# A vision tower in one kernel: one bf16 shift row per head, the range flag on VectorE, a rebuilt preparation, and embed and value projection in one piece each

## The chip, the core and the metric

The kernel runs on one core of one Trainium2 chip. The metric is the device time of one execution in microseconds, the median of several runs. One execution was recorded by the hardware profiler; what is said of durations comes from that record.

## What is computed

Sixteen images of 128 x 512 numbers are cut into 1024 patches of 64, embedded, passed through one attention layer with a bias per column, and through a mixture of eight experts of which each token takes two. Cut to what matters:

```python
h = patches(x) @ W.T + b + pos_embed              # 16 x 1024 x 64
y = layernorm(h)
q, k, v = y @ Wq + bq, y @ Wk + bk, y @ Wv + bv   # 8 heads of 8
col_bias = zeros(8, 1024).at[:, edge_index[1]].set((edge_attr @ We + be).T)   # the last edge of a node wins
attn = softmax(q @ k.T / sqrt(8) + col_bias[None, :, None, :])
h = h + (attn @ v) @ Wo + bo
t = layernorm(h)
p = softmax(t @ router_w.T); keep the two largest, divide by their sum
h = h + t + sum_e combine[:, e] * (gelu(t @ w1[e] + b1[e]) @ w2[e] + b2[e])
```

A softmax does not change when a number is subtracted from all scores of a row. The kernel makes use of that: it subtracts a bound (the shift) in place of the row's maximum, and has a slow path for an image whose bound is too large to be safe (its flag).

## The kernel before

The program has three stages: the **setup** (lines 720 to 1070), the **main loop** over 16 images, and the **expert stage** (64 units of work, four per image).

**Main loop.** An image is 32 quads. In quad q TensorE makes four score matmuls of 128 x 512 (`scores`, L1446: keys against queries, four heads, in two blocks of 1024 columns), ScalarE takes the exponential of both blocks (L1247), and TensorE multiplies the probabilities of quad q-2 by the values (`values`, L1462, four groups of 32 columns of the array side by side). The blocks go through three score buffers in PSUM, so a block's scores wait for the exponential of three blocks before. All other work of TensorE is put between the two, at most one piece in a quad: the table `AUX_SLOTS` names the quad, the step and its half. Pieces are the projection of queries and keys of the next image (`qk0`, `qk1`), the output projection, router and combine weights of the image before (`out_proj`, `post_t`, `router`, `combine_t`), the sums of squares of queries and keys (`sq`), the flag, the values of the next image (`v`), and embedding and transposition of the image after the next (`embed`, `norm_t`). All pieces write the same PSUM bank `aux`. So each step waits until VectorE has emptied the bank of the step before (`aux_drained`, in `aux_step`), and a waiting piece holds up the scores and values that stand behind it on TensorE.

VectorE runs its steps in the same order of quads (`body`, from L1355). Its own work sits at named quads: `evacuate` at quads 1, 9, 17 and 25 (it turns the summed values, L1315, and divides them, for the output projection), `centre_tokens` at 7, `scale_tokens` at 9, `rank_experts` at 20, `weigh_experts` at 22, `lead_centre` at 25, `normalise` at 27. `scale_tokens` waits for GpSimd, which takes the power -1/2 (L1187).

**The operands of the scores.** A score matmul has 54 rows: 48 hold the bf16 parts of queries and keys (three parts each, six products), three hold the column bias against ones, three hold the shift of the query (in three bf16 parts) against ones. Per image VectorE splits queries and keys into parts (L513 to L523), makes the shift of each query from its sum of squares and its head's bounds (`shift_of`, L536 to L553), SyncE stores parts and shift in DRAM and reads them back as rows (`store_parts`, `store_shift`, `load_rows`, `load_shift`). The flag of an image comes from a matmul over the heads (L697) and VectorE (L505); TensorE, ScalarE and VectorE read it when an image begins.

**Setup.** The winning edge of each node is found by matmuls of one-hot codes: VectorE makes `hot_b` and `hot_a` by 32 instructions each (L939, L942), TensorE sums them (L1047, 128 matmuls), VectorE finds the winners (L955 on), GpSimd gathers their attributes (L888). VectorE makes the bias, TensorE turns it (L1065), VectorE splits it into parts (L1023 on); ScalarE's queue stores the parts in DRAM and reads them as rows of `KA` (L845 to L851). GpSimd clears the values' tile `VA` (L877). The first image's embedding, projections and parts are made between these. At the end of the setup all engines meet.

```python
        dict(embed_0=7, embed_1=6, norm_t_0=2, qk0=3, qk1=4, v=7, sq=3, norm_t_1=2, flag=6)   # banks in the setup
```

Of the kernel before, what the change touches and what calls it, by code (L numbers as in the profile page):

```python
# [11 lines left out]
P = 128  # L12
# [40 lines left out]
HALVED = ["qk0", "qk1", "out_proj", "router", "v", "embed"]  # L53
LEAD = ["embed", "norm_t"]
PREP = ["qk0", "qk1", "v", "sq", "flag"]
POST = ["out_proj", "post_t", "router", "combine_t"]
FIRST_STEPS = ["embed_0", "embed_1", "norm_t_0", "qk0", "qk1", "v", "sq", "norm_t_1", "flag"]
FIRST_DRAINS = ["embed_0", "embed_1", "qk0", "qk1", "v", "sq", "norm_t_1", "flag"]
CENTRE_SLOT, SCALE_SLOT, LEAD_SLOT, NORM_SLOT = 7, 9, 25, 27
ROUTER_EXP_BLOCK = 38  # L60
# [61 lines left out]
def attention(nc, pool, io, psum, scratch, out):  # L122
    H_all, bmax, ident, ident_bf = (pool[k] for k in ("H_all", "bmax", "ident", "ident_bf"))
    q_parts_d, k_parts_d, shift_d, fb_d = (scratch[k] for k in ("q_parts", "k_parts", "shift", "fb"))
    x2_d, cT_d = scratch["x2"], scratch["cT"]
    ctx = ExitStack()
    with ctx:
# [58 lines left out]
        ones8 = sb("ones8", [H, 1], F32)  # L186
# [16 lines left out]
        sq = sb("sq", [P, BANK], F32)  # L203
# [5 lines left out]
        rq = sb("rq", [H, 1], F32)  # L209
        coef = sb("coef", [P, 4], F32)  # L210
        excess = sb("excess", [H, 1], F32)
        shift = sb("shift", [Q_ROWS, BANK], F32)
        shift_rest = sb("shift_rest", [Q_ROWS, BANK], F32)
        shift_parts = sb("shift_parts", [Q_ROWS, PARTS, BANK], BF16)
# [14 lines left out]
        def last_use(k):  # L229
# [6 lines left out]
                      dict(embed_0=7, embed_1=6, norm_t_0=2, qk0=3, qk1=4, v=7, sq=3, norm_t_1=2, flag=6).items()}  # L236
# [31 lines left out]
        excess_ready = sem("excess_ready")  # L268
# [3 lines left out]
        shift_stored = sem("shift_stored")  # L272
# [25 lines left out]
        EDGE_CHAIN = 25  # L298
        AUG_DMAS = 2 * 2 + 2
        PARTS_STORES = 16 * 12  # L300
        FB_SCORED, FB_MAXED, FB_MOVED, FB_CHAIN = FB_UNITS + 1, FB_UNITS + 1, 48, 4
        LEAD_CHAIN, PREP_CHAIN, POST_CHAIN, EVAC_CHAIN = 3, 13, 20, 5
# [20 lines left out]
        def sync_steps(sp):  # L323
# [1327 lines left out]
```

## Time and profile before

| | |
|---|---|
| median of 3 runs | 1176.12 us (1175.19 to 1176.16) |
| the profiled execution | 1175.44 us |
| its span, first to last instruction | 1173.6 us |
| TensorE matmul busy | 1105.3 us (94%) |
| ScalarE busy | 1030.7 us (88%) |
| VectorE busy | 671.2 us (57%) |
| GpSimd busy | 131.8 us (11%) |
| first scores of the main loop | at 55.5 us |
| last exponential of the main loop starts | at 1009.9 us |

The span is what the parts of the argument add up in; 1.84 us of the profiled execution lie around it. A busy TensorE here isn't TensorE at its limit, since it counts from the start of a matmul to its modelled end and the matmuls overlap. ScalarE's exponentials overlap as well. So the views in order of time say more than the shares.

### The profile page before, as it was taken

The page shows a single profiled execution, that of the slowest core. Times are in us where ns is not written, and L with a number is a line of the kernel's source. Part 1 is how long each engine was busy: PE and PEld are TensorE (multiplying, and loading weights), DVE is VectorE, ACT ScalarE, POOL GpSimd, SP SyncE. Part 2 cuts the span into 40 slices and gives each one's busy share as a digit, 9 for nine tenths or more (in the row PEclk, how much of TensorE's full clock was granted, in tenths as well). Part 3 has the DMA queues.
Part 4 walks back from the last instruction along what each step waited for, and adds up shares of the span by engine and source line. Part 5 has one row for each costly group of instructions (what it writes and reads, how often), then busy time and mean ns, then how long its engine had stood idle before and what let it go on. Part 6 is the DMA issues. An engine that isn't in the chain of part 4 may idle for free. (4 is left out here: it accounts for less than half of the span.)

```text
span 1173.6 us, 21907 instructions
## 1 busy us (share of the span) xinstructions
PE 1105.3 (94%) x7938; PEld 326.1 (28%) x7938; DVE 671.2 (57%) x1899; ACT 1030.7 (88%) x1127; POOL 131.8 (11%) x137
## 2 busy tenths in 40 slices
PE   3399999999999999999999999999999999899998
PEld 3122222222222222222222222222222222233332
DVE  9542756565656555565656565656565624367665
ACT  0199999999999999999999999999999999754553
POOL 4302201010101010101010101010101100000000
PEclk8589999999999999999999999999999999999999
DMA  2421323232323232323232323222222220022332
GB/s 52 111 74 39 85 53 82 53 83 53 83 53 84 53 83 53 83 49 87 49 88 49 86 50 73 63 68 67 62 67 55 72 61 10 16 63 66 84 75 50
DMA packets 63041, 75.93 MB, mean 65 GB/s; under 512 B 26338, under 2 KB 31458, under 8 KB 62906
## 3 DMA queue, kind: packets, MB, share of 16 engines
q1 hardware_dynamic: 60076, 73.01, 25.1%
q8 instruction: 80, 1.31, 0.5%
q10 hardware_dynamic: 2350, 1.10, 0.4%
q14 instruction: 55, 0.45, 0.1%
q0 software_dynamic: 480, 0.06, 0.1%
HBM read 37.54 MB, written 36.49 MB: 63 GB/s over the span
## 5 line engine op out<-in xcount | busy, mean ns | idle before, releaser
L1247 ACT ACTIVATE probs<-psum 128x1024 f32<-128x1024 f32 x1024 | 946.5, 1144 | 13.2 <-PE psum L1446 10.9
L1462 PE MATMUL psum<-probs,VA 128*32 128x512 f32 x4096 | 547.0, 606 | 5.3 <-DVE oT L1315 0.9
L1446 PE MATMUL psum<-QA,KA 54*128 54x512 bf16 x2048 | 331.7, 385 | 20.0 <-ACTq L1266 9.1
L1446 PEld LDWEIGHTS psum<-QA,KA 54*128 54x128 bf16 x2048 | 75.0, 93 | 491.5 <-ACT probs L1247 448.3
L1315 DVE STREAM_TRANSPOSE oT<-psum 128x512 f32<-128x512 f32 x64 | 45.9, 717 | 143.3 <-PE psum L1462 143.3
L1462 PEld LDWEIGHTS psum<-probs,VA 128*32 128x32 f32 x4096 | 82.1, 108 | 144.6 <-issue 86.1
L1282 ACT ACTIVATE probs<-psum,b 128x1024 f32<-128x1024 f32 x64 | 67.9, 1111 | 53.6 <-PE psum L1515 53.5
L1393 DVE TENSOR_TENSOR probs<-probs,psum 128x1024 f32<-128x1024 f32 x64 | 78.2, 1221 | 51.6 <-PE psum L1525 30.4
L484 DVE TENSOR_SCALAR qk<-psum,b_qk,scale_qk 128x512 f32<-128x512 f32 x32 | 25.8, 810 | 134.4 <-PE psum L673 134.4
L1515 PE MATMUL psum<-m_x,w 64*128 64x512 f32 x256 | 60.5, 591 | 1.5 <-ACT probs L1282 1.5
L1539 PE MATMUL psum<-probs,w 128*64 128x512 f32 x256 | 60.9, 598 | 0.0
L395 POOL COPY VA<-v_new 128x256 f32<-128x256 f32 x32 | 12.7, 397 | 426.1 <-DVE v_new L489 270.6
L1187 POOL TENSOR_TENSOR p_rstd<-p_ve,neg_half 128x8 f32<-128x8 f32 x16 | 32.3, 2020 | 230.5 <-DVE p_ve L430 230.5
L386 POOL TENSOR_TENSOR rstd<-ve,neg_half 128x8 f32<-128x8 f32 x16 | 31.6, 1974 | 123.4 <-DVE ve L430 123.4
L673 PE MATMUL psum<-xnT,w_qk 64*128 64x256 f32 x128 | 39.2, 407 | 0.8 <-ACT xnT L839 0.8
L1525 PE MATMUL psum<-m_cT,spread 64*128 64x512 bf16 x128 | 24.7, 382 | 6.4 <-DVE probs L1393 6.3
L661 PE MATMUL psum<-w_tok,xT 128*128 128x128 f32 x128 | 24.0, 317 | 6.7 <-DMA tok_b<-in_tok_b 6.7
L1515 PEld LDWEIGHTS psum<-m_x,w 64*128 64x128 f32 x256 | 24.3, 188 | 19.2 <-issue 15.2
L459 DVE TENSOR_TENSOR H_all<-psum,posb 128x512 f32<-128x512 f32 x16 | 11.1, 692 | 29.3 <-PE psum L661 29.2
L1289 ACT ACTIVATE yT<-psum 128x512 f32<-128x512 f32 x16 | 9.6, 597 | 20.2 <-PE psum L1539 20.2
L673 PEld LDWEIGHTS psum<-xnT,w_qk 64*128 64x128 f32 x128 | 24.7, 204 | 8.3 <-issue 1.9
L1320 DVE TENSOR_TENSOR oT_norm<-oT,o_inv 128x128 f32<-128x128 f32 x64 | 24.9, 389 | 2.3 <-DVE o_inv L1318 0.2
(175 smaller groups left out, 830.9 us busy)
## 6 DMA issues: line engine op xcount, KB each, us to landing
QA<-q_parts_d SPq DMA_DIRECT2D x64, 192.0 KB
KA<-k_parts_d SPq DMA_DIRECT2D x64, 192.0 KB
q_parts_d<-qk_parts SPq DMA_DIRECT2D x31, 192.0 KB, 2.5
k_parts_d<-qk_parts SPq DMA_DIRECT2D x31, 192.0 KB, 2.7
xT<-in_xT SPq DMA_DIRECT2D x16, 256.0 KB, 2.6
x_d<-x2T SPq DMA_DIRECT2D x16, 256.0 KB, 2.1
m_x<-x_d SPq DMA_DIRECT2D x16, 256.0 KB, 2.7
out_h<-result SPq DMA_DIRECT2D x16, 256.0 KB, 3.2
```

Source lines behind the costliest of these rows:

```text
L386: g.tensor_tensor(rstd[:, :], ve[:, :], neg_half[:, :], ALU.pow).then_inc(rstd_ready, 1)
L484: v.tensor_scalar(qk[:, n * BANK:(n + 1) * BANK], bank, b_qk[:, 0:1], scale_qk[:, 0:1], ALU.add, ALU.mult).then_inc(free, 1)
L673: last = pe.matmul(aux[:, cols], w_qk[rows, :, :].rearrange("k a e -> k (a e)"), xnT[rows, cols], start=True, stop=True)
L1187: g.tensor_tensor(p_rstd[:, :], p_ve[:, :], neg_half[:, :], ALU.pow).then_inc(p_rstd_ready, 1)
L1247: nc.scalar.activation(probs[:, k % PROB_BUFS, :], score_buf(buf_of(k)), ACT.Exp).then_inc(exped, 1)
L1282: nc.scalar.activation(act_h[:, u % H_BUFS, :], hid[u % 2], ACT.Gelu, bias=b1[:, u % PAIRS:u % PAIRS + 1]).then_inc(gelued, 1)
L1315: v.transpose(oT[:, :, :].rearrange("p j r -> p (j r)"), o_acc).then_inc(o_evacuated, 1)
L1393: v.tensor_tensor(gated[:, u % H_BUFS, :], act_h[:, u % H_BUFS, :], wgt, ALU.mult).then_inc(gated_ready, 1)
L1446: last = pe.matmul(score_buf(buf_of(k))[:, (g % 2) * BANK:(g % 2 + 1) * BANK], KA[rows_of(h, SCORE_ROWS), h // 2, jt * P:(jt + 1) * P], QA ...
L1462: last = pe.matmul(o_acc[32 * g:32 * g + 32, :], VA[:, jt, h, :], probs[:, k % PROB_BUFS, (g % 2) * BANK:(g % 2 + 1) * BANK], start=(jt == ...
L1515: last = pe.matmul(hid[u % 2][:, t * BANK:(t + 1) * BANK], w1[rows, m, :], m_x2[rows, b % 2, :], start=True, stop=True)
L1539: last = pe.matmul(ysum[D * t:D * (t + 1), :], w2[:, m, :], gated[:, u % H_BUFS, t * BANK:(t + 1) * BANK], start=False, stop=(m == PAIRS - 1))
```

## The change

- **Shift.** One bf16 number per head in place of three parts per query: minus the product of the largest norms of queries and keys of the head, not under -32. `shift_of` is one instruction on 8 x 1024, behind it `flag_of` makes the flag with a 32 x 32 transpose, a maximum and a comparison. Both stand at quad 14 on VectorE, behind quad 12's `sq`. The copy of the sums of squares, the shift's arithmetic and splitting, its round trip through DRAM and the flag's matmul are gone. `load_shift` copies the row from SBUF to SBUF, `load_zeros` writes zeros in the other two rows.
- **Quads.** The table of pieces and VectorE's own quads are changed; `embed` and `v` have one piece in place of two.
- **Setup.** The one-hot codes are made by three instructions over 4096 elements per partition. ScalarE clears `VA`. The bias's largest value is subtracted from the bias itself before it is split (`bias_tops`, `bmax`, `bias_low`), and its parts go from SBUF to the rows of `KA` directly, three DMAs on each of two queues (`place_bias`). The parts of heads 4 to 7 of the first image are stored in the main loop (`first_parts(sp, 1)`). Eight matmuls of 128 x 512 that nobody reads stand at the end of TensorE's setup, and TensorE waits for the bias's rows ahead of the loop.

```diff
-AUX_SLOTS = {0: ("qk0", 0), 1: ("qk0", 1), 2: ("qk1", 0), 4: ("qk1", 1), 6: ("out_proj", 0), 7: ("out_proj", 1),
-             10: ("sq", 0), 13: ("post_t", 0), 16: ("router", 0), 18: ("router", 1), 19: ("flag", 0), 20: ("v", 0),
-             21: ("v", 1), 23: ("embed", 0), 24: ("embed", 1), 26: ("combine_t", 0), 29: ("norm_t", 0)}
+AUX_SLOTS = {0: ("qk0", 0), 2: ("qk0", 1), 4: ("qk1", 0), 6: ("qk1", 1), 8: ("out_proj", 0), 10: ("out_proj", 1),
+             12: ("sq", 0), 14: ("post_t", 0), 16: ("router", 0), 18: ("router", 1), 21: ("embed", 0), 25: ("v", 0),
+             28: ("combine_t", 0), 30: ("norm_t", 0)}
-CENTRE_SLOT, SCALE_SLOT, LEAD_SLOT, NORM_SLOT = 7, 9, 25, 27
-ROUTER_EXP_BLOCK = 38
+CENTRE_SLOT, SCALE_SLOT, SHIFT_SLOT, LEAD_SLOT, NORM_SLOT = 10, 12, 14, 23, 26
+ROUTER_EXP_BLOCK = 40
-COMBINE_SLOT, WEIGH_SLOT = 20, 22
+COMBINE_SLOT, WEIGH_SLOT = 20, 25
...
+            def load_shift(bp, hg):
+                sp.wait_ge(shift_ready, bp + 1)
+                for par in range(2):
+                    r = HALF_ROWS * par + SHIFT_ROW
+                    heads = slice(4 * hg + par, 4 * hg + 4, 2)
+                    sp.dma_start(QA[r:r + 1, 2 * hg:2 * hg + 2, :].rearrange("o h i -> o (h i)"),
+                                 shift_row[heads, :]).then_inc(aug_loaded[hg], 16)
...
+            def shift_of(bp, st):
+                v.wait_ge(rq_ready, bp + 1)
...
+                v.tensor_scalar(shift_row[:, :], minus_ones[:, :], rq[0:H, 0:1], -RQ_CLIP, ALU.mult,
+                                ALU.max).then_inc(shift_ready, 1)
...
-                    for n in range(32):
-                        v.tensor_scalar(hot_b[:, n, :], node_bf[:, :], float(n), exp_bits[:, 0:1].bitcast(F32),
-                                        ALU.is_equal, ALU.mult)
-                    for n in range(32):
-                        last = v.tensor_scalar(hot_a[:, n, :], node_af[:, :], float(n), None, ALU.is_equal)
-                    last.then_inc(hot_ready, 1)
+                    each = digits[:, :, :].unsqueeze(1).broadcast_to([P, EC // 2, 32, 2])
+                    in_pairs = "p (m t) -> p m t"
+                    nodes_b = node_bf[:, :].rearrange(in_pairs, t=2).unsqueeze(2).broadcast_to([P, EC // 2, 32, 2])
+                    nodes_a = node_af[:, :].rearrange(in_pairs, t=2).unsqueeze(2).broadcast_to([P, EC // 2, 32, 2])
+                    link(v.tensor_tensor(hot_b[:, :, :, :], nodes_b, each, ALU.is_equal))
+                    v.tensor_scalar(hot_b[:, :, :, :], hot_b[:, :, :, :], exp_bits[:, 0:1].bitcast(F32), None, ALU.mult)
+                    v.tensor_tensor(hot_a[:, :, :, :], nodes_a, each, ALU.is_equal).then_inc(hot_ready, 1)
+                    v.memset(ones3[:, :], 1.0).then_inc(ones_ready, 1)
+                    v.memset(zeros[:, :], 0.0).then_inc(ones_ready, 1)
...
-                    g.wait_ge(hot_ready, 1)
-                    g.memset(VA[:, :, :, :], 0.0).then_inc(room_set, 1)
...
+                    for n in range(WARM_MATMULS):
+                        pe.matmul(first_bank["qk1"], ident_bf[:, :],
+                                  hot_b[:, 0:8, :, :].rearrange("p m b t -> p (m b t)"), start=True, stop=True)
...
+                pe.wait_ge(bparts_moved, 96)
                 all_batches(pe, body)
```

What moved, at the three places of which the prediction speaks. First, **VectorE around quads 9 to 13** of an image (`oT`, `o_inv` and `oT_norm` are the evacuation, `h` the output projection, `x` and `H_all` `scale_tokens`, `sq_max` the emptying of the bank after `sq`). Before:

```order
L430 TENSOR_SCALAR p_ve<-p_mv 128x8
L433 TENSOR_TENSOR p_centred<-h,p_mv 128x512
L1315 STREAM_TRANSPOSE oT<-psum 128x512
L1318 RECIPROCAL o_inv<-oT 128x16
L1320 TENSOR_TENSOR oT_norm<-oT,o_inv 128x16x8
L574 TENSOR_TENSOR x<-p_centred,p_rstd 128x2x4x64
L576 TENSOR_TENSOR H_all<-h,x 128x512
L498 COPY sq<-psum 128x512
L499 TENSOR_REDUCE sq_max<-psum 128x1
```

Now:

```order
L1314 STREAM_TRANSPOSE oT<-psum 128x512
L1317 RECIPROCAL o_inv<-oT 128x16
L1319 TENSOR_TENSOR oT_norm<-oT,o_inv 128x16x8
L575 TENSOR_TENSOR h<-psum,H_all 128x512
L419 BN_STATS p_stats<-h 128x6 x8
L425 BN_AGGR p_mv<-p_stats 128x2 x8
L427 TENSOR_SCALAR p_ve<-p_mv 128x8
L430 TENSOR_TENSOR p_centred<-h,p_mv 128x512
L563 TENSOR_TENSOR x<-p_centred,p_rstd 128x2x4x64
L565 TENSOR_TENSOR H_all<-h,x 128x512
L495 TENSOR_REDUCE sq_max<-psum 128x1
```

The output projection stands behind the evacuation of quad 9 now, and `scale_tokens` straight in front of `sq`'s maximum; the copy of `sq` is gone. Before, the maximum stood there too, but the output projection was three quads earlier.

Second, **TensorE at quads 20 to 24** before (each quad is four scores, a piece or none, and values; `w_v` marks `v`, `w_tok` marks `embed`):

```order
L1446 MATMUL psum<-QA,KA 128x512 x4
L677 MATMUL psum<-w_v,xnT 128x128 x2
L1462 MATMUL psum<-probs,VA 32x512 x4
L1446 MATMUL psum<-QA,KA 128x512 x4
L677 MATMUL psum<-w_v,xnT 128x128 x2
L1462 MATMUL psum<-probs,VA 32x512 x4
L1446 MATMUL psum<-QA,KA 128x512 x4
L1462 MATMUL psum<-probs,VA 32x512 x4
L1446 MATMUL psum<-QA,KA 128x512 x4
L661 MATMUL psum<-w_tok,xT 128x128 x2
L1462 MATMUL psum<-probs,VA 32x512 x4
L1446 MATMUL psum<-QA,KA 128x512 x4
```

and at quads 25 to 28 now:

```order
L1448 MATMUL psum<-QA,KA 128x512 x4
L666 MATMUL psum<-w_v,xnT 128x128 x4
L1464 MATMUL psum<-probs,VA 32x512 x4
L1448 MATMUL psum<-QA,KA 128x512 x4
L1464 MATMUL psum<-probs,VA 32x512 x4
L1448 MATMUL psum<-QA,KA 128x512 x4
L1464 MATMUL psum<-probs,VA 32x512 x4
L1448 MATMUL psum<-QA,KA 128x512 x4
L696 MATMUL psum<-ident_bf,comb_parts 128x128 x4
L1464 MATMUL psum<-probs,VA 32x512 x4
```

`v` is one piece of four matmuls with two quads without a piece behind it, and `combine_t` follows in the third.

Third, **VectorE behind the router**, where the experts' weights are made (`rank` is the last of the ranking, the weights begin with `chosen` and end, ten instructions later, in `comb_parts`). Before, at quads 21 and 22:

```order
L626 TENSOR_REDUCE rank<-above 128x64
L489 TENSOR_TENSOR v_new<-psum,b_v 128x512
L632 SCALAR_TENSOR_TENSOR chosen<-rank,rprob 128x64
L634 TENSOR_REDUCE c_sum<-chosen 128x8
L635 TENSOR_SCALAR c_inv<-c_sum 128x8
L636 RECIPROCAL c_sum<-c_inv 128x8
```

Now, at quad 25:

```order
L1314 STREAM_TRANSPOSE oT<-psum 128x512
L1317 RECIPROCAL o_inv<-oT 128x16
L1319 TENSOR_TENSOR oT_norm<-oT,o_inv 128x16x8
L486 TENSOR_TENSOR v_new<-psum,b_v 128x512
L621 SCALAR_TENSOR_TENSOR chosen<-rank,rprob 128x64
L623 TENSOR_REDUCE c_sum<-chosen 128x8
L624 TENSOR_SCALAR c_inv<-c_sum 128x8
```

The weights (`chosen` and the ten instructions behind it) stood behind the `v` of quad 21, ahead of the evacuation of quad 25; they stand behind that evacuation now.

## Rows read from the trace of the kernel before

**Rows 1.** The page, clock of TensorE in 40 slices, tenths of full speed

```profile
PEclk8589999999999999999999999999999999999999
```

**Rows 2.** Timeline of ScalarE, image 5: start, us, engine, line, what, count [idle before]

```profile
404.02 17.52 ACT L1247 ACTIVATE probs<-psum 128x1024 f32<-128x1024 f32 x19 [0.24 <-PE psum L1446]
```

**Rows 3.** The exponentials' own view: duration ns shortest/median/longest, first and last start

```profile
L1247 ACT ACTIVATE probs<-psum x1024: 1017/1136/1581, 56.2 to 1009.9; 128x1024 f32<-128x1024 f32 x171
```

**Rows 4.** Timeline of GpSimd, the same step in two images after each other

```profile
373.70 2.02 POOL L1187 TENSOR_TENSOR p_rstd<-p_ve,neg_half 128x8 f32<-128x8 f32 x1 [11.54 <-DVE p_ve L430]
...
433.25 2.02 POOL L1187 TENSOR_TENSOR p_rstd<-p_ve,neg_half 128x8 f32<-128x8 f32 x1 [11.54 <-DVE p_ve L430]
```

**Rows 5.** Timeline of TensorE, image 5, quads 21 to 25

```profile
395.53 0.60 PE L1446 MATMUL psum<-QA,KA 54*128 54x512 bf16 x4
396.07 0.71 PE L677 MATMUL psum<-w_v,xnT 128*128 128x128 f32 x4
...
397.71 0.61 PE L1446 MATMUL psum<-QA,KA 54*128 54x512 bf16 x4
398.24 1.06 PE L1462 MATMUL psum<-probs,VA 128*32 128x512 f32 x8
399.24 0.60 PE L1446 MATMUL psum<-QA,KA 54*128 54x512 bf16 x4
...
403.59 0.39 PE L1446 MATMUL psum<-QA,KA 54*128 54x512 bf16 x2
```

**Rows 6.** Timeline of TensorE, image 5, a transposing piece

```profile
410.92 0.66 PE L667 MATMUL psum<-ident,xn 128*128 128x128 f32 x4
```

**Rows 7.** Timeline of VectorE, image 5, from the output projection to the combine parts

```profile
370.79 0.69 DVE L586 TENSOR_TENSOR h<-psum,H_all 128x512 f32<-128x512 f32 x1 [0.51 <-PE psum L701]
...
374.98 0.72 DVE L1315 STREAM_TRANSPOSE oT<-psum 128x512 f32<-128x512 f32 x1 [0.77 <-PE psum L1462]
...
376.34 0.68 DVE L574 TENSOR_TENSOR x<-p_centred,p_rstd 128x512 f32<-128x512 f32 x1
...
377.67 0.69 DVE L498 COPY sq<-psum 128x512 f32<-128x512 f32 x1
378.27 0.68 DVE L499 TENSOR_REDUCE sq_max<-psum 128x1 f32<-128x512 f32 x1
...
397.72 0.69 DVE L489 TENSOR_TENSOR v_new<-psum,b_v 128x512 f32<-128x512 f32 x1
398.33 0.22 DVE L632 SCALAR_TENSOR_TENSOR chosen<-rank,rprob 128x64 f32<-128x64 f32 x1
...
400.64 0.21 DVE L646 COPY comb_parts<-comb_parts 128x192 bf16<-128x192 bf16 x1
```

**Rows 8.** Timeline of all engines, the one-hot codes and what follows on them

```profile
3.65 5.30 DVE L939 TENSOR_SCALAR hot_b<-node_bf,exp_bits 128x128 bf16<-128x128 bf16 x32
...
8.86 3.35 DVE L942 TENSOR_SCALAR hot_a<-node_af 128x128 bf16<-128x128 bf16 x32
12.11 4.64 DVE L947 TENSOR_TENSOR posb<-posb,tok_b 128x512 f32<-128x512 f32 x1
...
12.27 4.61 PE L1047 MATMUL psum<-hot_b,hot_a 128*32 128x32 bf16 x128 [3.47 <-DVE hot_a L942]
...
19.63 1.22 DVE L955 SCALAR_TENSOR_TENSOR key<-psum,base 128x1024 int32<-128x1024 int32 x1
...
33.67 0.69 DVE L516 TENSOR_TENSOR squares<-qk_parts 128x1024 bf16<-128x1024 bf16 x1
```

**Rows 9.** Timeline of all engines, from the bias parts to the first scores

```profile
44.59 0.28 DVE L1023 CAST bparts<-psum 64x128 bf16<-64x128 f32 x1
...
49.48 0.62 SPq L360 DMA_DIRECT2D shift_d<-shift_parts  x2
...
55.53 1.04 PE L1446 MATMUL psum<-QA,KA 54*128 54x512 bf16 x4 [9.12 <-ACTq L1266]
```

**Rows 10.** Waits of ScalarE from 58 to 70 us: us in total, times, longest

```profile
ACT probs L1247 <- PE psum L1446: 2.8, 2, 1.9
```

More of the change, by code:

```diff
@@ L208, in attention @@
         rq2 = sb("rq2", [H, 1], F32)
[L209 to L214, printed above, removed]
+        rq = sb("rq", [32, 32], F32)
+        rq_turned = sb("rq_turned", [32, 32], F32)
+        rq_top = sb("rq_top", [1, 1], F32)
+        shift_row = sb("shift_row", [H, T], BF16)
         flags = sb("flags", [1, NB], I32)
@@ L502, in prep_step, with flag_of @@
                     square_bounds(link)
-                    shift_of(bp, link, close)
-                elif step == "flag":
-                    v.tensor_scalar(flags[0:1, ds(bp, 1)], bank[0:1, 0:1], 1.0, None,
-                                    ALU.min).then_inc(free, 1)
-                    v.wait_ge(free, freed)
-                    v.sem_inc(flag_ready, 1)
+            def shift_of(bp, st):
+                v.wait_ge(rq_ready, bp + 1)
+                if later(bp):
+                    for hg in range(2):
+                        v.wait_ge(aug_loaded[hg], 16 * AUG_DMAS * bp)
+                    alone(v)
+                v.tensor_scalar(shift_row[:, :], minus_ones[:, :], rq[0:H, 0:1], -RQ_CLIP, ALU.mult,
+                                ALU.max).then_inc(shift_ready, 1)
+            def flag_of(bp, st):
+                link, close = st["link"], st["close"]
+                link(v.transpose(rq_turned[:, :], rq[:, :]))
+                link(v.reduce_max(rq_top[:, :], rq_turned[0:1, 0:H], AX.X))
+                close()
+                v.tensor_scalar(flags[0:1, ds(bp, 1)], rq_top[:, :], RQ_LIMIT, None,
+                                ALU.is_gt).then_inc(flag_ready, 1)
             def split_high(bp, link):
+                if bp == 1:
+                    v.wait_ge(first_stored[1], PARTS_STORES // 2)
                 if bp > 1:
@@ L693, in aux_step @@
                                              squares[:, i * BANK:(i + 1) * BANK], start=True, stop=True)
-                elif step == "flag":
-                    pe.wait_ge(excess_ready, n + 1)
-                    alone(pe)
-                    last = pe.matmul(aux[0:1, 0:1], excess[:, :], ones8[:, :], start=True, stop=True)
                 elif step == "out_proj":
@@ L808, in _ @@
                     load_rows(0)
[L809 to L810 removed]
+                    place_bias(sp, 0)
                     sp.wait_ge(ones_placed, 64)
@@ L1047, in _ @@
                         last = pe.matmul(sums[tile:tile + 32, 32 * (m // 4):32 * (m // 4) + 32],
-                                         hot_a[:, :, m], hot_b[:, :, m], start=True, stop=True)
+                                         hot_a[:, m // 2, :, m % 2], hot_b[:, m // 2, :, m % 2], start=True, stop=True)
                         if m % 32 == 31:
@@ L1364, in body @@
                             scale_tokens(b - 1, st)
+                        if slot == SHIFT_SLOT and b + 1 < NB:
+                            shift_of(b + 1, st)
+                            flag_of(b + 1, st)
                         if slot == LEAD_SLOT and b + 2 < NB:
```

217 lines of the change are left out of this document (99 added, 118 removed).

## The prediction

> **What bounds the kernel now.** I read the page first, then ScalarE in order of time, then TensorE and VectorE quad by quad, then the setup. In the main loop ScalarE is the bound. It ends an exponential every 0.916 us: 19 of them span 17.52 us, less the 1.02 that one takes alone, over 18 [rows 2, 3]. 64 of them are 58.62 us, and the image takes 59.55, the distance of one and the same GpSimd step in two images [rows 4]. So 0.93 us an image are lost; about 0.14 of that is the router's exponential, which stays, and the rest is ScalarE waiting for scores, as the 0.24 at quad 25 shows [rows 2].
>
> TensorE is close behind. A quad without a piece takes it 1.53 us (397.71 to 399.24), against 1.83 for ScalarE's two exponentials; with half a `v` it takes 2.18 (395.53 to 397.71), so half a piece costs 0.65 and an empty quad gives back 0.30 [rows 5]. How late may TensorE be? The two blocks' scores start 0.22 apart (four take 0.61, two 0.39), and an exponential starts 0.43 behind its scores (403.59 to 404.02) [rows 2, 5]. The second block's scores start when an old exponential ends; the next quad's first exponential has to end four steps, 3.66 us, later, so its scores must start 3.66 - 1.02 - 0.43 = 2.21 after that moment. TensorE would be there after 1.53 - 0.22 = 1.31. The **lead is thus 0.9, less about 0.05 for the signal: 0.85 us** (an estimate). What a piece or a wait takes beyond it, less 0.30 per empty quad, is lost to ScalarE for good. The same rule over all quads of the kernel before gives 0.84 an image where 0.93 are measured, so I add 0.09 to what it says below.
>
> Ahead of the loop stand 55.5 us of setup, a chain of steps. And TensorE runs at half its clock, 1.2 GHz, around the start of the loop (the 5 in the second slice) [rows 1], which leaves ScalarE waiting for 2.8 us in image 0 [rows 10].
>
> **Setup: one-hot codes.** Sixty-four instructions took 5.30 + 3.35 us [rows 8]. Now three go over 4096 elements each. A two-source bf16 instruction of 1024 elements takes 0.69 [rows 8]; with some 0.15 of start, 4096 take 2.3 us. For the product with one source, each of the 32 `hot_a` instructions took 0.105 for 128 elements, mostly start, so I take 1.2 and 2.3 as its other end. Sum 2.3 + 1.2 + 2.3 = 5.8, a gain of 2.9. The nearest row is of plain rows of memory, though, and these instructions read each pair of nodes 32 times over; were they to take one element per cycle, twice 2.1 us would come back (a rival below).
>
> The Trainium skill ("Vector Engine (DVE) Microarchitecture Reference", 5.1 Performance modes) has two-source instructions make two results a cycle if all types are 16-bit and the innermost dimension is dense with more than one element. A pair is such a dimension, so by the page the 2.3 stands; it also reports one element read again and again at one result a cycle, which is the rival's case.
>
> **Setup: the bank and the port.** `posb` took 4.64 us, beside GpSimd's clearing of `VA`; the same shape takes 0.69 elsewhere (`h`) [rows 7, 8]. ScalarE clears `VA` now, in time where it only waits. So the additions, the first embedding and its statistics fit beside TensorE's 4.61 us of sums: codes ready at 9.3, sums at 14.0, VectorE there at about 14.2 (some 1.5 for two memsets of 1536 elements in all, at the 512 in 0.69 of `h`; 0.7 for `posb`; 2.8 for the rest, as from its end at 16.75 to 19.63). `key`, at 19.63, starts **5.4 us earlier** [rows 8]. What follows on it, winners, gather, bias, is a chain without change up to one more copy (0.25) and then a maximum and a subtraction (0.65).
>
> **Setup: its end.** The parts began at 44.59 [rows 9]; now 44.59 - 5.4 + 0.25 + 0.65 = 40.1, done at 41.3. Before, shift arithmetic up to 49.48 and two hops through DRAM followed, 6.05 us to the first scores at 55.53 [rows 9]. Now one hop remains: three small DMAs per queue and a landing, some 3.3 us, 44.6; TensorE then reads the flag and branches, 1.1 us. First scores at 45.7, **a gain of 9.8**. The bounds are 7 (a hop of 4, codes late by 2) and 11.5. What SyncE's queue sheds from the setup, the parts of heads 4 to 7, is needed at quad 16, 29 us later: no cost. The eight spare matmuls take 3.4 at half clock and end by 44, behind the bias: no cost.
>
> **The clock at the start.** They may make the clock rise earlier. Bounds 0 and the 2.8 of [rows 10]; since TensorE idles for a microsecond or two behind them, and quads 0 and 1 hold no values, I take **1.0**.
>
> **Main loop: whole pieces.** Four matmuls in place of two add 0.44 to the 0.65 (four passes in the 0.71 of [rows 5], less 0.27 of the last): 1.09; the other bound is 2 x 0.65 = 1.30. Over the lead of 0.85 this loses 0.24 in quad 25. In quad 21 the router's exponential, just ahead on ScalarE, gives most of it back: 0.10. The losses of before (out_proj in adjacent quads, `v` in 20 and 21, `embed` in 23 and 24) go. Were this all, an image would gain some 0.4 us. The flag's matmul and the shift's arithmetic on VectorE were hidden: nothing.
>
> **Main loop: the wait in quad 14.** The bank must be emptied of `sq` before `post_t`, and on VectorE that maximum stands behind `scale_tokens`, which waits for GpSimd. Counted from quad 10's scores: evacuation of quad 9 begins at 0.2 (its values end about then: 1.06 from their start [rows 5]); +1.36 to `h`; +4.93 to the end of GpSimd's power (370.79 to 375.72); `x` at once and +1.33 to the next bank read; +0.68 and a signal: 8.55 [rows 4, 7]. Transposing and values add 0.6 and 1.0 [rows 5, 6]: quad 15's scores start 10.15 after quad 10's. Allowed are five quads, 9.16, plus the lead left, 0.85 - 0.65 + 0.30 = 0.50. **Lost 0.5.** Before, the bank was free three quads earlier. Queued behind the waiting piece are two quads' values and scores, hence ScalarE.
>
> **Main loop: quads 26 to 28.** From quad 26's scores, which have no lead after `v`: the evacuation begins at 0.2; its transpose (0.72) frees the sums at 1.0, so quad 27's scores come at 2.0, not 1.83: 0.18 lost. Then 1.36 for the evacuation, 0.61 `v_new`, 2.52 for the weights [rows 7]: `comb_parts` at 4.7. The piece (0.4) and values (1.0) bring quad 29's scores to 6.1; allowed are 2.0 + 3.66. **Lost 0.45.**
>
> Together 0.10 + 0.24 + 0.5 + 0.18 + 0.45 + 0.14 + 0.09 = 1.70, against 0.93: **+0.8 us an image**. Thirteen images have all of it, 10.4; image 14 (no embedding) about 0.9, image 0 (nothing of an image before) -0.2: **+11.1**. The expert stage is untouched.
>
> **Sum.** 1173.6 - 9.8 - 1.0 + 11.1 = 1173.9 of span, with the 1.84 around it 1175.7, against 1175.44 of the profiled execution and 1176.12 as median: no change. About 0.2% (2.35 us) is what a measurement of this kernel can tell from none.
>
> **Rivals.**
> - *The two waits don't bite.* If VectorE came 0.8 us sooner at both places, only the whole pieces would count: 1175.4 - 10.8 - 14 x 0.4 = 1159. For it: nothing idle is on those chains but GpSimd's 2.02. Against: each term is a row. Chance 0.07; half of it (1168) 0.13.
> - *The waits run longer.* TensorE's whole pieces at 1.30 add 0.2 twice an image, or signals on the chains 0.2 more each: +5.6, 1181.3. It decides as soon as an image takes over 60.5 us. Chance 0.17.
> - *One-hot codes at one element per cycle*: +4.2, 1179.9, if both comparisons take over 4 us each. Chance 0.08.
> - *The clock rises with the spare matmuls and stays*: -1.8 and a faster end of setup, 1173. Chance 0.12.
>
> My own case has 0.43. Its bounds and the rivals give 1168 to 1182; I hold the low end at 1170, leaving out the first rival. Faster 0.34 (the first and fourth rival and some of my case), same 0.38, slower 0.28.
>
> **What would show it.** First scores near 45.7; the three code instructions 2.3, 1.2, 2.3; `posb` 0.7; the same GpSimd step 60.3 apart in two images; `post_t` on TensorE waiting some 0.9 for VectorE's `sq_max`, and `combine_t` some 0.8 for `comb_parts`. An image of 59.2 would refute the waits; first scores after 48 would refute the setup.

## The result, and the profile after

| | before | after |
|---|---|---|
| median | 1176.12 us (1174.67 to 1176.65, 11 runs) | 1178.47 us (1178.12 to 1179.55, 11 runs) |
| ratio to before | | 1.0025, 95% interval 1.0017 to 1.0032 |
| the profiled execution, its span | 1175.44, 1173.6 us | 1178.41, 1176.3 us |
| first scores, first exponential | 55.53, 56.18 | 47.16, 47.59 |
| image 0, from its first exponential's end to the next image's | 62.54 | 60.75 |
| an image of the main loop | 59.55 | 60.51 |

The change is slower by 0.25%, a little more than the 0.2% within which I had called it no change (1175.7). The time is inside the range.

**Setup.** The timeline of the changed kernel, all engines (start us, us, engine, line, what); it answers to [rows 8]:

```profile
3.79 2.29 DVE L930 TENSOR_TENSOR hot_b<-node_bf,digits 128x4096 bf16<-128x4096 bf16 x1
...
6.11 1.29 DVE L931 TENSOR_SCALAR hot_b<-hot_b,exp_bits 128x4096 bf16<-128x4096 bf16 x1
...
7.32 2.28 DVE L932 TENSOR_TENSOR hot_a<-node_af,digits 128x4096 bf16<-128x4096 bf16 x1
...
9.65 1.29 PE L1042 MATMUL psum<-hot_b,hot_a 128*32 128x32 bf16 x128 [0.83 <-DVE hot_a L932]
...
11.13 0.62 DVE L938 TENSOR_TENSOR posb<-posb,tok_b 128x512 f32<-128x512 f32 x1
...
14.63 1.22 DVE L946 SCALAR_TENSOR_TENSOR key<-psum,base 128x1024 int32<-128x1024 int32 x1
```

The codes take 5.86 us in place of 8.65, `posb` 0.62 in place of 4.64, and `key` starts at 14.63, 5.0 us earlier (14.2 was predicted). TensorE's 128 matmuls on the codes take 1.29 us, where they took 4.61 before [rows 8]. How `posb` lay among its neighbours before (the same view of the kernel before) matters for the account below:

```profile
12.27 4.49 PEld L1047 LDWEIGHTS psum<-hot_b,hot_a 128*32 128x32 bf16 x128 [3.77 <-DVE hot_a L942]
...
12.34 5.81 POOL L877 MEMSET VA<- 128x2048 f32 x1 [9.43 <-DVE hot_a L942]
...
16.79 0.69 DVE L459 TENSOR_TENSOR H_all<-psum,posb 128x512 f32<-128x512 f32 x1
```

Then the end of the setup, which answers to [rows 9]:

```profile
41.09 0.28 DVE L1024 TENSOR_TENSOR bparts<-b_rest,bparts 64x128 bf16<-64x128 f32 x1
...
41.41 2.10 ACTq L778 DMA_DIRECT2D KA<-bparts  x3
...
47.16 0.61 PE L1448 MATMUL psum<-QA,KA 54*128 54x512 bf16 x4 [3.08 <-issue]
...
47.59 5.61 ACT L1246 ACTIVATE probs<-psum 128x1024 f32<-128x1024 f32 x6 [23.76 <-PE psum L1448]
```

and the view of the tile `bparts` (duration ns shortest/median/longest, first and last start; then the time from issue to landing):

```profile
L778 ACTq DMA_DIRECT2D KA<-bparts x3: 602/613/822, 41.4 to 42.9; - x3
...
DMA to landing us min/median/max: 2.5/2.8/3.2
```

The parts are ready at 41.4 as predicted. The last of the six small DMAs is issued at 42.9 and lands 2.6 later, at 45.5, and the first scores come 1.6 behind that: 5.8 us from the parts to the scores, where I had 4.4.

**The clock.** The page's row, against [rows 1]:

```profile
PEclk9699999999999999999999999999999999999999
```

The 6 is the slice from 29.4 to 58.8 us. In it the granted clock is at half from 30.6 to 44.2 and again from 47.7 to 54.5 us: TensorE starts the loop at full clock, falls back within a microsecond, and is back for good at 54.5.

**Main loop.** GpSimd's step in two images, which answers to [rows 4], is 60.51 apart:

```profile
372.39 2.02 POOL L1185 TENSOR_TENSOR p_rstd<-p_ve,neg_half 128x8 f32<-128x8 f32 x1 [17.23 <-DVE p_ve L427]
...
432.90 2.02 POOL L1185 TENSOR_TENSOR p_rstd<-p_ve,neg_half 128x8 f32<-128x8 f32 x1 [17.23 <-DVE p_ve L427]
```

The timeline of ScalarE over image 5 shows where it loses time. Behind each bracket ScalarE waited for scores; a run of x11 exponentials takes 10.19, which is 0.916 for each but the last:

```profile
378.67 10.19 ACT L1246 ACTIVATE probs<-psum 128x1024 f32<-128x1024 f32 x11 [0.56 <-PE psum L1448]
388.63 0.36 ACT L1251 ACTIVATE router_e<-logits 128x64 f32<-128x64 f32 x1
388.78 12.50 ACT L1246 ACTIVATE probs<-psum 128x1024 f32<-128x1024 f32 x13
401.44 3.77 ACT L1246 ACTIVATE probs<-psum 128x1024 f32<-128x1024 f32 x4 [0.17 <-PE psum L1448]
405.52 10.19 ACT L1246 ACTIVATE probs<-psum 128x1024 f32<-128x1024 f32 x11 [0.31 <-PE psum L1448]
```

The distances of the ends of the exponentials, quad by quad, less 2 x 0.916, as a mean of images 1 to 13:

```
quad      7    14   19/20  21   23   24   25   26   28   sum
before  0.15    -   0.14  0.23 0.05 0.34   -    -    -   0.91
after     -   0.67  0.14  0.12   -    -  0.25 0.27 0.42  1.87
```

The waits of the changed kernel (us in total, times, longest), the two of the prediction among them:

```profile
PE psum L672 <- DVE sq_max L495: 12.4, 14, 1.0
...
PE psum L696 <- DVE comb_parts L635: 8.8, 14, 0.6
...
PE psum L1464 <- DVE oT L1314: 7.7, 16, 0.5
```

`post_t` (L672) waits 0.87 an image for `sq_max`, and `combine_t` (L696) 0.63 for `comb_parts`: both new waits are there. The chain to quad 14 in image 5, TensorE and then VectorE:

```profile
367.92 0.61 PE L1448 MATMUL psum<-QA,KA 54*128 54x512 bf16 x4
...
376.69 0.63 PE L672 MATMUL psum<-ident,x 128*128 128x128 f32 x4 [0.87 <-DVE sq_max L495]
377.24 1.07 PE L1464 MATMUL psum<-probs,VA 128*32 128x512 f32 x8
378.24 0.60 PE L1448 MATMUL psum<-QA,KA 54*128 54x512 bf16 x4
```

```profile
368.13 0.72 DVE L1314 STREAM_TRANSPOSE oT<-psum 128x512 f32<-128x512 f32 x1 [1.12 <-PE psum L1464]
...
369.49 0.68 DVE L575 TENSOR_TENSOR h<-psum,H_all 128x512 f32<-128x512 f32 x1
...
374.52 0.69 DVE L563 TENSOR_TENSOR x<-p_centred,p_rstd 128x512 f32<-128x512 f32 x1 [1.61 <-POOL p_rstd L1185]
...
375.85 0.68 DVE L495 TENSOR_REDUCE sq_max<-psum 128x1 f32<-128x512 f32 x1
```

From quad 10's scores (367.92) to quad 15's (378.24) it is 10.32; I had 10.15. And quads 25 to 29, TensorE and then VectorE:

```profile
396.82 1.16 PE L666 MATMUL psum<-w_v,xnT 128*128 128x128 f32 x8
...
398.91 0.61 PE L1448 MATMUL psum<-QA,KA 54*128 54x512 bf16 x4
400.01 1.06 PE L1464 MATMUL psum<-probs,VA 128*32 128x512 f32 x8 [0.50 <-DVE oT L1314]
401.01 0.60 PE L1448 MATMUL psum<-QA,KA 54*128 54x512 bf16 x4
...
403.78 0.38 PE L696 MATMUL psum<-ident_bf,comb_parts 128*128 128x128 bf16 x4 [0.63 <-DVE comb_parts L635]
...
405.09 0.60 PE L1448 MATMUL psum<-QA,KA 54*128 54x512 bf16 x4
```

```profile
399.15 0.72 DVE L1314 STREAM_TRANSPOSE oT<-psum 128x512 f32<-128x512 f32 x1 [2.33 <-PE psum L1464]
...
403.42 0.21 DVE L635 COPY comb_parts<-comb_parts 128x192 bf16<-128x192 bf16 x1
```

### The profile page after: what moved, and what is told of

It is laid out like the page before. It is cut to its first block and busy times, and to the rows that moved or that the text cites. A ratio compares the mean times of both kernels' runs of the same rounds, so it can differ in the third digit from the quotient of the medians.

```text
span 1176.3 us, 21673 instructions
## 1 busy us (share of the span) xinstructions
PE 1093.9 (93%) x7913; PEld 319.5 (27%) x7914; DVE 611.9 (52%) x1700; ACT 1033.8 (88%) x1127; POOL 126.8 (11%) x137
## 3 DMA queue, kind: packets, MB, share of 16 engines
q8 instruction: 79, 1.29, 0.5%
## 5 line engine op out<-in xcount | busy, mean ns | idle before, releaser
L1517 PE MATMUL psum<-m_x,w 64*128 64x512 f32 x256 | 60.5, 591 | 1.5 <-ACT probs L1281 1.5
L462 DVE COPY xnT<-psum 128x512 f32<-128x512 f32 x15 | 10.4, 690 | 47.4 <-PE psum L656 47.4
L597 DVE TENSOR_REDUCE r_sum<-router_e 128x8 f32<-128x64 f32 x16 | 3.5, 220 | 54.0 <-ACT router_e L1251 54.0
L650 PE MATMUL psum<-w_tok,xT 128*128 128x128 f32 x128 | 20.4, 307 | 7.5 <-DMA tok_b<-in_tok_b 6.7
```

Source lines behind the costliest of these rows:

```text
L1517: last = pe.matmul(hid[u % 2][:, t * BANK:(t + 1) * BANK], w1[rows, m, :], m_x2[rows, b % 2, :], start=True, stop=True)
```

## The experiments

Each is the changed kernel with the edit named; the ratio is to the kernel before, run beside it on the same chip. In the first four only quads are changed. The kernel before took 1176.64 us beside e1 to e4, 1176.13 beside e5 to e8 and 1176.00 beside e9 to e11, so a difference of medians across these groups, or to the changed kernel's 1178.47, holds to about half a microsecond.

| | edit | median us | ratio, 95% interval | an image |
|---|---|---|---|---|
| e1 | `scale_tokens` a quad later | 1169.56 | 0.9940, 0.9924 to 0.9957 | 59.84 |
| e2 | `weigh_experts` a quad earlier | 1174.93 | 0.9985, 0.9976 to 0.9995 | 60.20 |
| e3 | quads of before | 1166.34 | 0.9908, 0.9892 to 0.9925 | 59.55 |
| e4 | `embed`, `v` in halves again | 1178.72 | 1.0022, 1.0013 to 1.0032 | 60.50 |
| e5 | no spare matmuls | 1179.12 | 1.0024, 1.0015 to 1.0034 | 60.49 |
| e6 | wait for the bias behind the flag | 1177.72 | 1.0014, 1.0004 to 1.0023 | 60.49 |
| e7 | a piece in every second quad | 1154.72 | 0.9816, 0.9800 to 0.9832 | 58.81 |
| e8 | e7 and e6 | 1153.53 | 0.9808, 0.9791 to 0.9824 | 58.81 |
| e9 | e8, bias parts leave one by one | 1153.79 | 0.9809, 0.9793 to 0.9825 | 58.81 |
| e10 | e9, 16 spare matmuls | 1154.71 | 0.9818, 0.9802 to 0.9835 | 58.81 |
| e11 | e8 again, beside e9 and e10 | 1152.99 | 0.9805, 0.9789 to 0.9821 | 58.81 |

My theory was that the new quads cost about 0.8 us an image through two waits and the whole pieces, and that the setup gives 9 to 10 back. The rivals were that the whole pieces alone cost it, and that the loss has to do with the new shift on VectorE.

**e1, the wait in quad 14.**

```diff
-CENTRE_SLOT, SCALE_SLOT, SHIFT_SLOT, LEAD_SLOT, NORM_SLOT = 10, 12, 14, 23, 26
+CENTRE_SLOT, SCALE_SLOT, SHIFT_SLOT, LEAD_SLOT, NORM_SLOT = 10, 13, 14, 23, 26
```

> The changed kernel with scale_tokens at quad 13 in place of 12, so that on VectorE the bank of sq is emptied ahead of it. In the changed kernel's profile an image takes 60.5 us and quad 14 loses 0.67 of that. Theory (TensorE's post_t waits for VectorE's sq maximum, which waits behind scale_tokens for GpSimd): the wait of post_t on sq_max goes, an image takes 59.8, the kernel about 9 us less (1169.5), and quads 25 to 28 keep their loss. Rival A (the transposing piece itself is what loses, whatever it waits for): an image stays at 60.5, 1178.5. Rival B (post_t then waits as long for x2, which GpSimd delays): a wait of some 0.8 for x2, 60.4.

`sq_max` stands ahead of `scale_tokens` on VectorE now, so the bank is empty before GpSimd's power is. TensorE's `post_t` has no idle time before it any more:

```profile
373.89 0.66 PE L672 MATMUL psum<-ident,x 128*128 128x128 f32 x4
```

The loss at quad 14 is 0, all others are as they were, and the time is 8.9 us shorter. The two profiles' spans differ by 8.7: images 1 to 14 are 9.65 shorter together, and in this profile the setup ended 0.8 later and image 0 took 0.15 more. So this wait alone costs about 9 us.

**e2, the wait in quad 28.**

```diff
-COMBINE_SLOT, WEIGH_SLOT = 20, 25
+COMBINE_SLOT, WEIGH_SLOT = 20, 24
```

> The changed kernel with weigh_experts at quad 24 in place of 25, ahead of the evacuation. Theory (combine_t in quad 28 waits for comb_parts, which stand behind evacuation and v): the wait on comb_parts goes, but v's bank and the evacuation may come later by what the weights take, so an image gains 0.2 to 0.4 us (60.1 to 60.3), the kernel 3 to 6 us (1172.5 to 1175.5). Rival (quads 25 to 28 lose because v is in one piece): an image gains nothing, 1178.5.

The 0.42 of quad 28 is gone and the time is 3.5 us shorter. Of the 0.42, 0.12 comes back at quad 26, since the weights stand ahead of the evacuation now and values wait longer for the transpose of the sums (`oT`, 7.7 before):

```profile
PE psum L1464 <- DVE oT L1314: 9.2, 16, 0.7
```

**e3, the quads of before** (table and VectorE's quads as before the change, the new shift at quad 11, the new setup kept).

```diff
+AUX_SLOTS = {0: ("qk0", 0), 1: ("qk0", 1), 2: ("qk1", 0), 4: ("qk1", 1), 6: ("out_proj", 0), 7: ("out_proj", 1),
+             10: ("sq", 0), 13: ("post_t", 0), 16: ("router", 0), 18: ("router", 1), 20: ("v", 0), 21: ("v", 1),
+             23: ("embed", 0), 24: ("embed", 1), 26: ("combine_t", 0), 29: ("norm_t", 0)}
+CENTRE_SLOT, SCALE_SLOT, SHIFT_SLOT, LEAD_SLOT, NORM_SLOT = 7, 9, 11, 25, 27
...
```

> The changed kernel (its setup, shift row and flag) with the quads of the kernel before, VectorE's own included, the shift at quad 11, v and embed in two pieces. Theory (the quads alone cost the main loop about 0.95 us an image; shift and setup only gain): an image back at 59.5, the kernel 1164 to 1167, which is 9 to 12 us under the kernel before. Rival (the shift row's DMAs, or the flag on VectorE, cost time in the main loop): an image stays above 60, 1174 or more.

Setup, shift and flag together are worth about 10 us: 10.3 against the kernel before beside it (1176.64 less 1166.34), 9.8 against its first median (1176.12). The image is 59.55 to the hundredth, with the losses of before in their old quads. So the shift and the missing flag matmul cost and bring nothing in the loop, and the new quads cost the other 12.1 (1178.47 less 1166.34), net of what they bring in image 0.

**e4, two pieces in place of one** (`embed` at 20 and 21, `v` at 24 and 25).

```diff
-             12: ("sq", 0), 14: ("post_t", 0), 16: ("router", 0), 18: ("router", 1), 21: ("embed", 0), 25: ("v", 0),
+             12: ("sq", 0), 14: ("post_t", 0), 16: ("router", 0), 18: ("router", 1), 20: ("embed", 0), 21: ("embed", 1),
+             24: ("v", 0), 25: ("v", 1),
-HALVED = ["qk0", "qk1", "out_proj", "router"]
+HALVED = ["qk0", "qk1", "out_proj", "router", "v", "embed"]
```

> The changed kernel with embed in quads 20 and 21 and v in quads 24 and 25, two pieces each, which end in the same quads as the whole pieces, so VectorE's order is the same. Theory (a whole piece costs 1.09 against 1.30 for two halves, but in one quad; both lose about as much over a lead of 0.85): an image within 0.2 of 60.5, the kernel 1176 to 1181. Rival (putting them in one piece is what costs): an image 0.5 or more shorter, 1171 or less.

Quad 21 loses 0.23 in place of 0.12 and quad 25 0.15 in place of 0.25: the sum is the same. One piece or two in adjacent quads makes no difference, which rules out the first rival. Whether it is their neighbourhood that counts, this run can't say; e7 takes them apart.

**e5, without the spare matmuls** (`WARM_MATMULS` 8 to 0).

> The changed kernel without the eight spare matmuls. Theory (they raise TensorE's clock for the loop's first microseconds, where the changed kernel lost 1.3 us in image 0 against 3.1 before): the granted clock is 1.2 GHz from the first scores on, image 0 takes 61.5 to 62.5 in place of 60.75, and since the engines meet perhaps 0.3 us sooner, the kernel is 0.5 to 1.5 us longer (1179.0 to 1180.0). Rival (qk0's second half moved out of quad 1 is what image 0 gained): image 0 stays at 60.8, the kernel at 1178.5 or under.

Image 0 takes 61.20, not 61.5 or more. The total is in the expected range but can't be told from the changed kernel's (ratios 1.0024 and 1.0025). Image 0 loses 0.46 more than in the changed kernel's profile, at quads 3 and 4. That isn't shown to be the spare matmuls' doing: in e2, which has all eight and the same first quads, image 0 takes 61.20 too and loses the same 0.46 there. In this trace the granted clock reads 1.00 throughout, though the matmuls tell otherwise; its first record of the clock is at 56.3 us, and the view shows what lies ahead of it as full:

```profile
52.59 1.94 PE L1464 MATMUL psum<-probs,VA 128*32 128x512 f32 x8
54.46 1.04 PE L1448 MATMUL psum<-QA,KA 54*128 54x512 bf16 x4
55.42 1.48 PE L1464 MATMUL psum<-probs,VA 128*32 128x512 f32 x8
56.84 0.60 PE L1448 MATMUL psum<-QA,KA 54*128 54x512 bf16 x4
```

Eight matmuls of values took 1.94 where they take 1.06 later, and four scores 1.04 where they take 0.60 two quads on: half clock, up to about 56.3. In the changed kernel the scores at 47.16 were at full pace, 0.21 apart, the granted clock was at half from 47.7 to 54.5, and then full. In the runs with the new first quads, what goes with the loss at quads 3 and 4 is how late the clock comes back behind the first values: 2.0 to 2.9 us in the changed kernel, e4, e6, e8 and e11, which lose 0.05 or nothing there, 3.1 and 3.4 in e1 and e7 (0.15 and 0.29), and 3.7 in e2 and e5 (0.46). All of these but e5 have the eight spare matmuls.

**e6, the wait for the bias behind the read of the flag.**

```diff
                     flag = pe.value_load(flags[0:1, ds(b, 1)], min_val=0, max_val=1)
+                    if b == 0:
+                        pe.wait_ge(bparts_moved, 96)
...
-                pe.wait_ge(bparts_moved, 96)
                 all_batches(pe, body)
```

> The changed kernel with TensorE's wait for the bias's rows moved behind its load of image 0's flag. In the changed kernel the last rows land at 45.5, and TensorE loads the flag and branches for 1.6 us behind that, first scores at 47.2. Theory (that order is most of the 1.4 us by which the end of the setup was sized too small): first scores near 46.0, the kernel 1.0 to 1.4 us less (1177.2). Rival (TensorE would wait as long for other loads or ScalarE): first scores at 47.2 again, 1178.5.

The first scores start at 46.36, 0.54 behind the last landing in place of 1.64. So 1.1 us of the start was TensorE's wait for the flag and its reading of it, which could as well run ahead of the wait for the bias; the branch on the flag still stands behind both, in the 0.54. By the medians 0.75 us of it arrived. In the profiles the first scores are 0.8 earlier, since the landing itself was at 45.82, 0.3 later than in the changed kernel's. The ratios' intervals overlap (1.0004 to 1.0023, and 1.0017 to 1.0032), so the clearer measure is e8 against e7 on one chip, 1.2.

**e7, a piece in every second quad**, and e8, the same with the late wait.

```diff
+             12: ("sq", 0), 14: ("post_t", 0), 16: ("router", 0), 18: ("router", 1), 20: ("v", 0), 22: ("v", 1),
+             24: ("embed", 0), 26: ("embed", 1), 28: ("combine_t", 0), 30: ("norm_t", 0)}
+HALVED = ["qk0", "qk1", "out_proj", "router", "v", "embed"]
+CENTRE_SLOT, SCALE_SLOT, SHIFT_SLOT, LEAD_SLOT, NORM_SLOT = 10, 13, 14, 27, 29
+COMBINE_SLOT, WEIGH_SLOT = 20, 23
```

> The changed kernel with a piece in every second quad: v in two pieces at quads 20 and 22, embed at 24 and 26, scale_tokens at 13, weigh_experts at 23, lead_centre at 27, normalise at 29. Theory (a half piece of 0.65 is inside the lead of 0.85 and the next quad gives back 0.30, and both of VectorE's late steps are gone): only the router's exponential is left, an image takes 58.8 to 59.0, the kernel 1153 to 1157. Rival (a loss that I do not know of comes in its place, a piece waiting for the bank of the piece two quads before): 59.4 or more, 1163 or more.

> The spaced quads together with the late wait. Theory: the two gains add, since one is in the setup and one in the loop: 1.0 to 1.4 us under the spaced kernel, 1152 to 1156. Rival (the two overlap, as image 0 waits for the slow clock anyway): as the spaced kernel.

By the rule of the prediction half a piece costs 0.65, within the lead of 0.85, and the empty quad behind it gives 0.30 back, so no quad should lose anything. ScalarE in image 5 of e7, start, us, count:

```profile
349.12 32.37 ACT L1246 ACTIVATE probs<-psum 128x1024 f32<-128x1024 f32 x35
381.07 0.55 ACT L1251 ACTIVATE router_e<-logits 128x64 f32<-128x64 f32 x1
381.22 31.59 ACT L1246 ACTIVATE probs<-psum 128x1024 f32<-128x1024 f32 x34
```

No idle time is left; only the router's exponential takes its 0.14. An image is 58.81, and the time is 21 us under the kernel before and 24 under the changed one; with the late wait another 1.2. The rule of the lead forecast this run (58.8 to 59.0 an image, 1153 to 1157 us), which is its strongest support. The run moves pieces and VectorE's steps at once, so it doesn't say what each move is worth.

**e9, the bias parts leave one by one** (to e8).

```diff
-                eng.wait_ge(bparts_ready, 1)
                 for a in range(PARTS):
+                    eng.wait_ge(bparts_ready, a + 1)
...
                     link(v.tensor_copy(bparts[:, 0, :], bias_low[:, :]))
+                    v.sem_inc(bparts_ready, 1)
...
                     link(v.tensor_copy(bparts[:, 1, :], b_rest[:, :]))
+                    v.sem_inc(bparts_ready, 1)
```

> The version with a piece in every second quad and the late wait, and each of the three bf16 parts of the bias leaves for KA as soon as VectorE has made it, in place of all three behind the last. In the changed kernel the parts are ready at 40.5, 41.1 and 41.4, the six DMAs are issued from 41.4 to 43.5, and the last lands at 45.5. Theory (the last hop is bound by issue of three DMAs in a row on each queue, 0.6 each, and then one landing of 2.6): issues from 40.6 on, the last by 42.7, lands at 44.7, first scores at 45.2, against 46.1: faster by 0.6 to 1.0, median 1152.5 to 1153.0. Rival (the landing is bound by something else, by the parts of the first image that are loaded at the same time): the last landing stays at 45.4 or later and the time within 0.3 of 1153.5.

The rival holds. The same view as above:

```profile
L778 ACTq DMA_DIRECT2D KA<-bparts x3: 602/638/770, 40.6 to 42.1; - x3
...
DMA to landing us min/median/max: 3.7/4.0/4.4
```

The DMAs are issued 0.8 us earlier and take 1.2 longer to land: the last lands at 45.87. The third part itself was ready 0.2 later than in the other runs, at 41.6, with two more signals ahead of it. The share of the DMA engines from 39 to 47 us, in slices of 0.2 us, in the changed kernel and in e9:

```profile
DMA  3885979999997999999865422110001989989989
```

```profile
DMA  3788959999999999999999982000001989989999
```

From about 40 the engines are full, to 43.0 us in the changed kernel and to 43.8 in e9, with the rows of `QA` and `KA` of the first image, four loads that SyncE issued from 37.6 to 40.2. The bias's own packets run from 42.6 to 44.35 in the changed kernel and from 42.95 to 44.0 in e9: so the 0.8 us of earlier issue is spent in waiting for the engines, as the rival has it. That the rows are the cause is read from this view, since the loads weren't taken away. But it isn't the whole hop. The engines are idle from 44.4 (44.0 in e9) to 45.0, and the last landing comes 1.2 us (changed kernel) and 1.85 us (e9) behind the bias's last packet. What that last stretch waits for no run shows.

**e10, 16 spare matmuls** (to e9).

> As the run with the early parts, and 16 spare matmuls in place of 8. With 8 the records show them 0.43 apart at half clock and 0.21 at full clock from 42.1 to 44.1 on, and the scores at half clock again from 47.5. Theory (the clock falls because TensorE does nothing between the spare matmuls and the first scores): 8 more take 1.7 to 3.4, so they end between 43.9 and 47.3; if they end at about 45, the four scores of quad 0 and on stay 0.21 apart, image 0 loses nothing at quad 2 (1.32 before), and the time is 0.8 to 1.3 shorter, 1151.3 to 1152.0. Rival (the clock falls again whatever is ahead of it, since the first two quads hold few matmuls): quad 2 loses over 1, and the spare matmuls delay the first scores by 0 to 2: 1152.5 to 1154.5.

The rival holds here too. TensorE in e10:

```profile
40.89 3.95 PE L1067 MATMUL psum<-hot_b,ident_bf 128*128 128x512 bf16 x15 [0.22 <-issue]
46.79 0.61 PE L1450 MATMUL psum<-QA,KA 54*128 54x512 bf16 x4 [1.94 <-ACTq L1267]
...
51.52 1.93 PE L1466 MATMUL psum<-probs,VA 128*32 128x512 f32 x8
```

The spare matmuls end at 44.8 and the first scores are at full pace, as in e9 (46.48). The granted clock falls again at 48.1 in e9 and at 48.8 in e10, ahead of the first values, and quad 2 loses 1.3 in both. The first scores are 0.3 later, and image 0 takes 60.79 against 60.60. Against e11 (image 0 60.12) both are slower by 0.8 to 1.7, so more of them is no gain. The difference of the three in image 0 is at quads 3 and 4 (0.48 in e9, 0.67 in e10, 0 in e11), and the clock comes back 3.8, 4.1 and 2.3 us behind the first values.

## Why the prediction was right or wrong

Term by term, in the span: what was predicted, and what the two profiles show.

| | predicted | measured |
|---|---|---|
| setup to the first exponential | -9.8 | -8.6 |
| image 0 | -1.2 | -1.8 |
| images 1 to 13 | +10.4 | +12.2 |
| image 14 | +0.9 | +1.35 |
| the rest | 0 | -0.5 |
| sum | +0.3 | +2.65 |

**Right: the mechanisms of the loop.** In the setup the durations up to the bias parts came about as worked out: codes 2.29, 1.29 and 2.28 against 2.3, 1.2 and 2.3, `posb` 0.62 against 0.7, parts done at 41.4 against 41.3. The codes read each pair 32 times over and were no slower for it: 4096 elements in 2.29 us is the pace of the 1024 in 0.69 [rows 8], and twice that of 512 f32 elements in 0.69 [rows 7]. By the Trainium skill's rule ("Vector Engine (DVE) Microarchitecture Reference", 5.1 Performance modes) such 16-bit operands make two results a cycle, and the trace agrees.

One term of the setup came right by luck, another for a reason that isn't shown. The 1.5 for the two memsets isn't what its row gives (1536 elements at 512 in 0.69 are 2.1); they took 0.91 and 0.48. And `posb` is short now, but that GpSimd's clearing had stretched it isn't shown. Before, it ended at 16.75, with TensorE's weight loads of the sums (12.27 + 4.49 = 16.76), while the clearing ran on to 18.15, and beside that clearing `H_all`, one of whose operands is in PSUM, took its usual 0.69. The change takes both neighbours away: ScalarE clears `VA`, and the new layout of the codes, in which the 32 numbers that a matmul reads from each partition lie 4 bytes apart in place of 256, went with sums of 1.29 us in place of 4.61, a term that the prediction had kept. No run separates the two. Nor did the shorter sums matter, since VectorE reaches `key` only at 14.63.

In the loop the six places of the losses are those named, the rule of the lead gives their sizes, and e1, e2 and e3 take away one after the other what it says. The rival of waits that don't bite is refuted by the 0.87 and 0.63 of idle time.

**Wrong: sizes, by three steps.** First, "one hop remains: three small DMAs per queue and a landing, some 3.3 us, 44.6; TensorE then reads the flag and branches, 1.1 us". The hop measured 4.1 and the start 1.64. Neither the 3.3 nor the 1.1 had a row behind it. I had taken the landing for the DMAs' own; e9 shows that the bias's packets wait for DMA engines that are full with the first image's rows, though the last 1.2 us to the landing stay open. That is 1.4 of the 9.8, of which a first exponential 0.43 behind its scores, in place of 0.65, gives 0.2 back.

Second, "lost 0.5" in quad 14, where it was 0.67. The chain was summed with `x` "at once" behind GpSimd's power and 0.05 for the signal to TensorE. The rows show 0.11 (372.39 + 2.02 to 374.52) and 0.16 (375.85 + 0.68 to 376.69), 0.22 more; the piece and the values then took 0.05 less than I had. Likewise at quad 26, where the evacuation begins 0.24 behind the scores in place of 0.2, and TensorE starts at 400.01, 0.14 behind the transpose's end at 399.87, in place of 0.08: 0.27 and not 0.18. Together that is 0.26 an image, less the 0.09 that I had added for what the rule didn't explain, which wasn't needed: with image 14, in which the same waits stand, 2.2 us. It is the second rival's mechanism ("signals on the chains 0.2 more each"), at 0.26 an image in place of its 0.4, about two thirds of its price of 5.6; only net of the 0.09 is it 2.2. That rival was to decide from 60.5 us an image, and the image is 60.51.

Third, the "1.0" for the clock. Image 0 gained 1.8, but most of it not by the clock: with the quads of before it takes 62.70 (e3), spare matmuls and all, and without the matmuls but with the new quads 61.20 (e5). At half clock scores and values alone take TensorE longer than ScalarE's 1.83 (from 52.59 to 55.42 in e5), a piece adds to it, and the new table spreads the first four pieces over quads 0 to 6. That is 1.3 to 1.5, and I had nothing for it: the 0.2 was for the pieces of later quads, which lose 0.80 in image 0 against 0.78 before. The other 0.3 to 0.5 goes with the clock's earlier return. That the spare matmuls bring it isn't shown, since e2 has them and takes 61.20 as well. They ended 3.1 us ahead of the first scores, not "a microsecond or two".

A sum of two terms of about ten with opposite signs was bound to hang on such tenths: that the time fell inside the range says little for the single terms. Of the 2.35 us that the forecast was short, the main loop makes 2.2, the setup 1.2, image 0 and the rest give 1.1 back.

## What to carry to other kernels

Where one engine is the bound and another feeds it with a small lead, write the lead down in us and give each piece of side work the quads it needs to be paid back: half a piece in every second quad cost nothing here, two in adjacent quads or one whole piece 0.1 to 0.4 each, and the pieces that waited 0.87 and 0.63 us cost 0.67 and 0.42, in each of 14 images. Count every hop between engines in such a chain (0.11 to 0.16 us here), since what is left over is of that size. And before a start is planned from issue times, look at what the DMA engines still have to move then, and put all that doesn't need the last data, such as reading a flag, ahead of the last wait.

## What was unexpected of the hardware

- The bias parts are ready at 41.35 to 41.40 us in ten of the twelve profiled executions with the new preparation; in e9 and e10, with their two more signals, at 41.6. The last landing behind it spreads from 45.52 to 46.26, and the first exponential, where the early wait stands, from 47.58 to 48.56. The changed kernel's own profile is one of the quickest; its 11 times lie in two groups, 1178.1 to 1178.5 and 1179.1 to 1179.6. One profile isn't enough to read tenths of a microsecond of a start.
- A small DMA from SBUF to SBUF (8 KB) took 2.5 to 3.2 us from issue to landing, and 3.7 to 4.4 when issued 0.8 us earlier into DMA engines that stayed full for longer; 1.2 to 1.85 us of it came behind its last packet.
- The granted clock can read full in a trace where matmuls run at half (e5, whose first record of the clock is at 56.3 us): there the durations decide.
- Of an f32 addition of 512 elements per partition that took 4.64 us before and 0.62 after, the end fell on that of TensorE's weight loads with a step of 256 bytes, and not on that of GpSimd's clearing. With a step of 4 bytes the same 128 matmuls took 1.29 us in place of 4.61. Which neighbour held it up no run shows.
